# A decoder layer: the first norm's statistics of the cross stage are formed by ScalarE in the self stage and handed over through DRAM

## What is computed

```python
x = x + attn_ref(layernorm(x), qkv_w, qkv_b, out_w, out_b)          # "self": per token, over the 4 batch rows
x = x + xattn_ref(layernorm(x), ctx, ctx, mask, Wq, ..., Wo, bo)    # "cross": 16 heads, 128 context rows
x = x + ffn_ref(layernorm(x), Win, bin, W1, b1, W2, b2, Wout, bout)
return x                                                            # x is [4, 2048, 512] float32
```

## Time and profile before

| | us |
|---|---|
| three runs | 1926.94, 1928.53, 1934.01 |
| median | 1928.53 |
| the profiled execution's own time | 1927.15 |
| its span (first to last instruction) | 1925.4 |
| TensorE clock over the span | 0.957 of full |

### The profile page before, as it was taken

The page is one execution under the profiler, slowest core; times in us unless marked ns, Lnnn a source line. Parts: engine busy times, 40 slices in busy tenths (PEclk is TensorE's granted clock), DMA queues, the critical chain, the costliest instruction groups (busy, mean ns, idle before and its releaser), DMA issues.

```text
span 1925.4 us, 39554 instructions
## 1 busy us (share of the span) xinstructions
PE 1711.4 (89%) x14016; PEld 1417.1 (74%) x14016; DVE 1554.3 (81%) x2268; ACT 1002.9 (52%) x3150; POOL 1012.0 (53%) x732
## 2 busy tenths in 40 slices
PE   5899999999999999836999898988988889989975
PEld 4678888888888888725777777776777777767764
DVE  5788888888888888864788887887888878878874
ACT  3432222233222233114688776776777767867771
POOL 3166666666666666653446543563446434644422
PEclk9999999999999999966999998998999989989997
DMA  5311111111111110130111111110111011101101
GB/s 197 100 55 45 44 44 44 44 44 44 44 44 44 47 52 29 35 118 23 41 41 63 32 44 59 58 63 14 58 58 51 30 53 58 64 19 58 36 18 44
DMA packets 55935, 99.05 MB, mean 51 GB/s; under 512 B 5312, under 2 KB 13632, under 8 KB 55744
## 3 DMA queue, kind: packets, MB, share of 16 engines
q1 hardware_dynamic: 53728, 94.12, 14.2%
q10 hardware_dynamic: 2016, 2.45, 0.4%
HBM read 59.59 MB, written 36.96 MB: 50 GB/s over the span
## 4 chain that ended last, share of the span: by engine, by line
PE 31%; DVE 14%; issue 6%; ACT 4%; POOL 1%; DVEq 1%; POOLq 0%; ACTq 0%
PE ring L1193 19%; PE sc L1221 4%; PE ring L1288 3%; DVE ntop L1398 3%; ACT prob_c L1325 2%; DVE stats_c L1436 2%; DVE x2T L1365 2%; PE ring L1246 1%; DVE stats L1405 1%; PE sc L1213 1%; PE ring L1198 1%; DVE x L1419 1%; DVE pT L1365 1%; DVE x L1455 1%; ACT x2T L1298 1%
## 5 line engine op out<-in xcount | busy, mean ns | idle before, releaser
L389 PE MATMUL qb<-wqkv,xT 128*128 128x512 f32 x2304 | 551.5, 393 | 6.1 <-DVE wqkv L802 6.1
L389 PEld LDWEIGHTS qb<-wqkv,xT 128*128 128x128 f32 x2304 | 429.4, 189 | 93.9 <-DVE wqkv L802 6.3
L1325 ACT ACTIVATE prob_c<-sc,ntop 128x128 f32<-128x128 f32 x1024 | 362.4, 391 | 153.5 <-DVE ntop L1398 153.5
L1148 POOL TENSOR_TENSOR rstd<-vare,half_c 128x1 f32<-128x1 f32 x64 | 35.0, 548 | 464.0 <-DVE vare L1412 464.0
L1325 ACT ACTIVATION_READ_ACCUMULATOR prob_c<-sc,ntop 128x1 f32 x1024 | 235.6, 230 | 0.0
L1193 PE MATMUL ring<-wqkv,aT_c 128*128 128x512 f32 x768 | 200.4, 411 | 39.6 <-DVE x L1419 39.6
L314 POOL TENSOR_TENSOR prod_pool<-v,prob 128x1024 f32<-128x1024 f32 x64 | 180.9, 2827 | 82.0 <-DVE prob L728 76.8
L1398 DVE TENSOR_REDUCE ntop<-sc 128x4 f32<-128x512 f32 x256 | 170.1, 687 | 49.9 <-PE sc L1221 36.3
L558 ACT ACTIVATE qk<-qb 128x512 f32<-128x512 f32 x128 | 76.3, 597 | 253.2 <-PE qb L389 253.2
L478 PE MATMUL ob<-wout,aT 128*128 128x512 f32 x768 | 191.7, 399 | 10.7 <-DVE aT L758 10.7
L1193 PEld LDWEIGHTS ring<-wqkv,aT_c 128*128 128x128 f32 x768 | 144.6, 195 | 75.2 <-DVE x L1419 35.9
(11 more groups left out here) (134 smaller groups left out, 3282.6 us busy)
## 6 DMA issues: line engine op xcount, KB each, us to landing
x_tile<-in_x SPq DMA_DIRECT2D x16, 1024.0 KB, 5.2
x_scratch<-xres SPq DMA_DIRECT2D x16, 1024.0 KB, 4.3
x_tile<-x_scratch SPq DMA_DIRECT2D x16, 1024.0 KB, 6.4
out<-x SPq DMA_DIRECT2D x64, 256.0 KB, 2.0
kt<-k_scratch SPq DMA_DIRECT2D x16, 512.0 KB, 3.2
v_c<-v_scratch SPq DMA_DIRECT2D x16, 256.0 KB, 4.3
raw<-in_wqkv SPq DMA_DIRECT2D x3, 1024.0 KB, 7.1
ctx<-in_ctx SPq DMA_DIRECT2D x1, 1024.0 KB, 7.7
```

Source lines behind the costliest of these rows:

```text
L389: last = nc.tensor.matmul(qb[g % 4][:, :], xT[p][a][:, k, t * P:(t + 1) * P], wqkv[b][:, k, c * D:(c + 1) * D], start=(n == 0), stop=(n == ...
L1325: last = nc.scalar.activation(prob[:, h, :], sc[g][:, (h % 4) * C:(h % 4 + 1) * C], ACT.Exp, bias=ntop[:, h:h + 1], accum_out=total[:, t % ...
```

## The change

The mean and 1/sqrt(var + EPS) of x1 are made in the self stage, in the layout of its tiles, stored as [R, S, 2] in a DRAM scratch and loaded with each x1 tile of the cross stage. ACT makes the sums: four passes `Copy` with an accumulator, a 4-column scaling by -1/512, four passes `Square` with the mean as bias and an accumulator, a 4-column `Copy` for var + EPS. POOL makes the power (128x4). Both work on tile j - 2 in step j; the self stage gets a step 17 for tile 15. POOL's residual of tile j, which overwrites the same `xres`, now waits for the last `Square` of tile j - 2. In the cross stage DVE's and POOL's statistics go away, and the norm adds the negated mean. `unused` takes the room of `raw0`, a buffer of the start.

```diff
-    for j in range(TILES - 3, TILES + 1):
+    for j in range(TILES - 3, TILES + 2):
         step(j, j % 2)
@@ SP, self stage, end of step j @@
...
+                        sp.wait_ge(st_out[q], 16 * ((TILES - 2) // 2))
...
+                    sp.dma_start(keep["st"][:, :, :],
+                                 st_dram[0, 0:R * P, :].rearrange("(t p) c -> p t c", p=P)).then_inc(keep["x1_in"], 16)
...
+                if has(j, -2):
+                    at = rows(j - 2)
+                    wait(sp, rstd1_done, j - 1)
+                    sp.dma_start(st_dram[:, at, :].rearrange("t p c -> p t c"), st[p][:, :, :]).then_inc(st_out[p], 16)
@@ POOL, self stage @@
+                if has(j, -2):
+                    wait(pool, var1_done, j - 1)
+                    nc.gpsimd.tensor_tensor(st[p][:, :, 1], vare1[:, :], half[:, :], ALU.pow).then_inc(rstd1_done, 1)
                 if has(j):
+                    wait(pool, ssq_done, R * (j - 1))
@@ ACT, self stage @@
+                def x1_sum(t):
...
+                    b = j - 2
+                    wait(act, x1_done, R * b + t + 1)
+                    wait(act, var1_done, b)
+                    nc.scalar.activation(unused[:, t, :], xres[p][:, t, :], ACT.Copy,
+                                         accum_out=sum1[:, t:t + 1]).then_inc(sum1_done, 1)
+                def x1_mean():
...
+                    nc.scalar.activation(st[p][:, :, 0], sum1[:, :], ACT.Copy, scale=-1.0 / D).then_inc(mean1_done, 1)
+                def x1_square(t):
...
+                    wait(act, mean1_done, b + 1)
+                    nc.scalar.activation(unused[:, t, :], xres[p][:, t, :], ACT.Square, bias=st[p][:, t, 0:1],
+                                         accum_out=ssq[:, t:t + 1]).then_inc(ssq_done, 1)
+                def x1_variance():
...
+                    nc.scalar.activation(vare1[:, :], ssq[:, :], ACT.Copy, scale=1.0 / D, bias=EPS).then_inc(var1_done, 1)
                 take(0)
+                x1_sum(0)
+                x1_sum(1)
                 take(1)
...
                 take(2)
+                x1_sum(2)
+                x1_sum(3)
+                x1_mean()
                 take(3)
+                x1_square(0)
+                x1_square(1)
...
                 for t in range(R):
                     take(R + t)
                     x_hi(t)
+                    if t < 2:
+                        x1_square(t + 2)
+                x1_variance()
@@ SP, cross stage @@
                     sp.dma_start(x1[:, :, :], x1_flat[at, :].rearrange("(t p) d -> p t d", p=P)).then_inc(x1_in, 16)
+                    sp.dma_start(st[:, :, :], st_flat[at, :].rearrange("(t p) c -> p t c", p=P)).then_inc(x1_in, 16)
@@ POOL, cross stage @@
-                    nc.gpsimd.tensor_tensor(xn[:, i % 2, :], x1[:, i, :], mv[:, i, 0:1].to_broadcast([P, D]),
-                                            ALU.subtract).then_inc(xm_done, 1)
+                    nc.gpsimd.tensor_tensor(xn[:, i % 2, :], x1[:, i, :], st[:, i, 0:1].to_broadcast([P, D]),
+                                            ALU.add).then_inc(xm_done, 1)
...
-                            wait(pool, var_done, 2 * (j + 1) + t + 1)
-                            nc.gpsimd.tensor_tensor(rstd[:, part], vare[:, part], half[:, part],
-                                                    ALU.pow).then_inc(rstd_done, 1)
-                            wait(pool, rstd_done, 2 * (j + 1) + t + 1)
-                            wait(pool, x1_in, 16 * (j + 2))
+                            wait(pool, x1_in, 32 * (j + 2))
@@ DVE, cross stage: the bn_stats part (L1434 to L1440) and the bn_aggr part (L1457 to L1463) of slots 0 and 1 are gone @@
```

More of the change, by code:

```diff
@@ L1385, in step @@
                 for t in range(R):
-                    two, one = active(j, "x2T", t), has(j, 1) and t < 2
-                    part = slice(2 * t, 2 * t + 2)
+                    two = active(j, "x2T", t)
                     over2 = TURNS_OVER["x2T"](j, t)
```

63 lines of the change are left out of this document (37 added, 26 removed).

## The result

The changed kernel takes 1924.85 us (median of 8 runs, 1923.11 to 1926.92), the kernel before, run beside it, 1929.38 us (8 runs, 1926.94 to 1934.01). The ratio is 0.9977, 95% interval 0.9968 to 0.9986: some 4.5 us or 0.23% faster. I had forecast 1915.5 us, 13 us under the median of before. The direction is right; two thirds of the gain is missing. The time lies inside the wide range, 1906 to 1930, and outside the forecast's own, 1909 to 1923. The change is less than the 0.5% that I had named as the least that can be told, though the interval leaves out 1.

The account below looks back on a forecast made before the run. PE bounds the self stage; the cross stage is a ring of hand-overs with no engine full. Cross slots -9.9, self stage 0, meeting of the stages -1.8: -11.7 from 1927.15 gives 1915.5 us, own range 1909 to 1923.

Parts of the forecast that it names:

- the wide range: Whole kernel: 1906 to 1930 us, leaving out the full chain and the paying self stage, together 0.18.
- Slot 0: First slot of a cross step: DVE's low part of x2T comes 0.56 us earlier, over 14 steps 7.8 us gained.
- Slot 1: Second slot of a cross step: removing the statistics gains 0.15 us, over 14 steps 2.1 us.
- the control in the same trace: Cross stage: slot 2 has slot 1's turns without statistics, 12.22 against 12.37 us, so statistics cost 0.15 us.
- Self stage: Self-stage steps: ACT's added passes and POOL's power do not make PE wait, 0 us.
- The cover I named: Self stage: DVE's idle gap of 2.25 us before the last `take_x1` takes up a load landing 0.2 us late.
- (a): End of self stage, step 17: last statistics, power and small store delay the cross block by 4.3 us (+3.5 to +7.5).
- (b): First norm of the cross block: POOL starts at once, PE's q products 11.6 us after block start, not 17.7: -6.1 us.
- the boundary term: Where self and cross stages meet: (a) +4.3 and (b) -6.1 together give -1.8 us, bounds -3 to +3.
- Nothing worth measuring: Rival: DVE's time is hidden in the cross stage, slot 0 gives 0 to 0.3 us; 1922 to 1928 us, chance 0.32.
- The chain pays in full: Rival: cross stage wins 1.9 us in slot 0 and 1.8 in slot 1, 14 times, 52 us: 1875; chance 0.08.
- The self stage pays: Rival: late ACT variance stalls POOL, then x loads, DVE's statistics and PE in the self stage; 1946 us, chance 0.10.

Follow-up runs that it names:

- 128-piece kernel: The changed kernel with a tile's statistics stored as 128 pieces of 32 bytes instead of 512 of 8, loads unchanged: 1917.79 us, ratio 0.9945.
- written-out kernels: The kernel before and the changed kernel, each with cross-stage steps 3 to 14 written out instead of looped: 1888.63 us (0.9794) and 1889.17 us (0.9795).
- four-step loop: The kernel before with its cross-stage hardware loop made of four steps in three passes instead of two steps in six: 1911.62 us, ratio 0.9903.

## Why the prediction was wrong

**Slot 0** (14 x 0.56 = 7.8 us). The size of one was right: 0.49 where no turn is ahead, from 11.42 to 10.94, with ACT's copy as the next to be late, as said. The count was wrong, and this is the first failed step. I took one steady step, an even one, for all fourteen. It stands for seven (3, 4, 6, 8, 10, 12, 14). Step 1 gains nothing, step 2 0.19. In the five odd steps behind a turn PE can be late. Timeline of DVE in slot 0 of step 9, changed kernel, then the matmuls of that projection in PE's timeline, changed, before, and in step 5 of the 128-piece kernel:

```profile
1456.61 0.69 DVE L1511 TENSOR_TENSOR x<-ring,xr 128x512 f32<-128x512 f32 x1 [1.66 <-PE ring L1257]
```

```profile
1452.66 3.82 PE L1257 MATMUL ring<-wqkv,aT_c 128*128 128x512 f32 x12
```

```profile
1451.85 3.01 PE L1193 MATMUL ring<-wqkv,aT_c 128*128 128x512 f32 x12
```

```profile
1190.67 3.02 PE L1261 MATMUL ring<-wqkv,aT_c 128*128 128x512 f32 x12
```

A freed DVE waits for these twelve matmuls, and how long they take is set by how far the stretch at 1.2 GHz behind the turn reaches into the slot: 2.4 to 5.8 us over all turns of the two-step loops. At full clock they take 3.0 us, else up to 4.4. In each of these odd steps the slot is 7.8 us longer than the matmuls, but not under 10.94 in the changed cross stage and 11.44 in the one with the statistics. So an odd step wins the whole 0.5 us when they take up to about 3.15 us, as in step 5 of the 128-piece kernel (10.94), and nothing from about 3.65 on. The two profiled executions differ in this by chance: 3.7 to 4.2 us in all five turns changed, 3.0 and 3.2 in two of the five before. That is why these steps gain nothing there. Over the other kernels with the change's cross stage the odd slots 0 are 10.9 to 11.8 us against 11.4 to 12.2 in the two with the statistics, some 0.3 us on average. So the term is 7 x 0.49 + 0.2 + 5 x 0 to 0.3 = 3.6 to 5.1 us and not 7.8. And the cause of the larger part of each 0.49 was named wrongly. I counted "0.65 of waiting and aggregates" with the statistics; the runs of the written-out kernels show that 0.29 of it is the looped form of a wait, which would go without any statistics being moved.

**Slot 1** (14 x 0.15 = 2.1 us). 12.37 to 12.22 in steps 3 to 14: right, the control in the same trace was worth its row. Steps 1 and 2 have nothing, so 1.8.

**Self stage** (0 us). Right. The cost of a pass is 0.61 to 0.71 us from start to start, under the 0.82 I took. POOL's power was costed at 1.02 us and takes 2.42 beside DVE in the self step shown (462.34), so the residual starts at 464.73 against 461.87 and SP's load at 472.07 against 470.44. The cover I named, DVE's gap ahead of the last `take_x1`, took it up: 483.09 with 2.26 of idle, in steps of 47.3 us. The kernel with only the self stage's part says the same.

**Where the stages meet, (a)** (+4.3 us). The second failed step. The step on ACT and POOL was right: from the last x1 to the end of the power I had 6.0 us, the trace 5.3 (856.49 to 861.77). Four squares took 2.84 us (started every 0.71 us) where the sum had 3.3 and the Trainium skill's "ScalarE: Activation LUTs", section "What ACT_TABLE_LOAD costs", made them 0.8 shorter than that; the trace lies between. The landing was the mistake: 7.7 us against the 2.5 of the sum. Part of it is the small store of the tile before, which lands only 1.3 us ahead of the last one; the sum had no term for that either. "The nearest row is the smallest store, 2.0 us" is a row of 256 KB in 128 large pieces; nearness in bytes was the wrong measure, and the upper bound, 5.2, was too low as well. 8.2 us was paid where 3.0 (2.5 and half a microsecond to the block) was in the sum. (a) is +8.8 us, counted from the last x1 to the block's start (5.34 and 14.18), against +4.3.

**(b)** (-6.1 us). Right: 17.73 to 11.42 us, -6.3.

**The sum.** Slot 0 3.6 to 5.1, slot 1 1.8, (a) +8.8, (b) -6.3: -2.9 to -4.4 us, against -4.5 measured, interval 2.7 to 6.2. The forecast of -11.7 was too high by 5.2 for the landing and by 3 to 4 for the count of slots. With the last landing of the 128 pieces, 1.4 us, under my estimate, the kernel takes 1917.79 us, 2.3 over the forecast; what is left of the miss is the count of slots. That the time fell inside the wide range does not speak for the sum: the boundary term, -1.8 us in the forecast, came out at +2.5.

**The rivals.** "Nothing worth measuring" gave the right time, 1925, for a wrong reason: slot 0 was to be worth 0.3 us at most, and (b) not more than (a). The second half of that is true. The rule of the Trainium skill that I set beside it ("Perfetto Trace Analysis", section "Identifying the Most-Contended Engine") doesn't bear on it as I had it: it warns that the matmul share is no measure for TensorE and takes the busy share of the weight loads instead. By that PEld has 752 us of 1040 and DVE 827, so DVE was the engine to relieve. Taking 45 us off DVE brought 4 to 6, and what helped most was a stretch in which no engine is busy, the turn. "The chain pays in full" and "The self stage pays" did not come about.

**What I could have seen.** The list of waits of the kernel before has the turn in it, five times:

```profile
DVE ntop L1398 <- PE sc L1221: 36.3, 8, 6.9
...
PE sc L1213 <- issue: 17.4, 5, 3.6
```

(waiting engine, line and cause; us in total, times, longest). A wait of 17.4 us in five pieces for "issue" ought to have been asked about before fourteen steps were taken to be alike.

## What to carry to other kernels

Before a saving is multiplied by the number of steps, list the lengths of all the steps: here every second one began behind a loop turn that cost 6 to 7 us and left PE at 1.2 GHz, and a saving on DVE reached it in part or not at all, as the clock came back. Price a small transfer by the size and number of its pieces and not by its bytes, and lay out a hand-over through DRAM so that a partition's numbers lie together; that edit alone more than doubled what the change brought. An experiment that takes away a wait shows only when the wait ends, and not whether the thing that was waited for still stands in someone's way.

## What the runs showed that I had not expected

- The hardware loop of the cross stage costs some 40 us of 1928. In the profiled pair steps 3 to 14 are 43 us shorter written out, 33 in the turns and 10 in the other slots. In those DVE shows 0.21 to 0.29 us of idle at a register wait behind its own statistics, and none written out; that all 10 us are such waits is not shown. A turn of the four-step loop is dearer (7.8 and 8.5 us) than one of the two-step loop (6.2 to 7.0). The self stage's loop costs nothing that the times show.
- The last store before the block's end, 4 KB in 512 pieces of 8 bytes, lands in 7.7 us, 8 KB in 512 pieces of 16 bytes in 3.5 (both with a store of their kind ahead), 4 KB in 256 pieces of 16 bytes in 2.4 and in 128 of 32 bytes in 1.4; loading 512 pieces of 8 bytes takes 6.4 to 7.8 (medians of the runs, each behind an x1 load), whatever the stores do.
- While such a store is under way, the issue of a small load on another engine's queue can take 4.00 us instead of 0.64, and that engine's next computing instruction stands behind it.
- POOL's power on 128x4 takes 2.42 us beside DVE's work in the steady self steps and 1.01 with DVE idle.
- A turn of the two-step loop comes with seven packets of instructions within 10 us (five in the changed kernel), and the even steps of the loop with none.
- What stays open: why 8 bytes are so much dearer than 16, whether the "issue" gaps at a turn are waits for those packets, why they grow with the loop's body, and why the last cross step differs by up to 2 us between executions.
